# Blocks 2 and 3 of the last but one state: scaled by ScalarE and added by the adding transfer

## The chip, the cores and the metric

One core of a Trainium2 chip runs the whole program in one launch. Five engines work from queues of their own, each in order: TensorE (PE, matrix products and transposes, with weight loads PEld), VectorE (DVE), ScalarE (ACT), GpSimd (POOL) and SyncE (SP, which only issues transfers). They wait for each other through semaphores. The metric is device microseconds of one execution; smaller is better.

## What is computed

Four layers, each added to its input after a layer norm: attention, a dense layer with fp8 rounding, a selective state-space layer, and a mixture of eight experts with a shared one. The input is 16 sequences of 512 positions by 256 features. The change touches the state-space layer, in whose scan 512 inner channels carry 16 states each:

```python
def _selective_scan(u, delta, A, B_ssm, C_ssm):
    dA = jnp.exp(delta[..., None] * A)
    dBu = (delta * u)[..., None] * B_ssm[:, :, None, :]
    ...
    def step(h, inp):
        dA_i, dBu_i, c_i = inp
        h = dA_i * h + dBu_i
        y = jnp.einsum('bds,bs->bd', h, c_i)
        return (h, y)
    ...
y = _selective_scan(u, delta, A, B_ssm, C_ssm)
y = y + u * D_param
y = y * _silu(z)
out = y @ out_proj_w.T + out_proj_b
```

## The kernel before

**Turns.** One turn works on one sequence b: 16 states s, and for each state four scans m (128 channels by 512 positions each), so 64 scans n = 4s + m. Inside a turn's scans three streams of other work are woven in by a table of slots (AT): the late part of sequence b - 1 (its output projection, router and shared expert), the projections of b + 1, and the attention and fp8 layer of b + 2. What a stream has left over at the end of a turn is issued behind the last scan. A second program, the experts, follows the 16 turns.

**One state.** GpSimd multiplies dbu (L914) from du and a row of B that SyncE brings in; ScalarE takes the exponential into a bank (L1134); VectorE runs the scan h (L1505). When a state's four scans are done, TensorE transposes h into four blocks t of 128 positions by 512 channels (L697, called hT s.t), in banks 4 and 5 in turn: blocks 0 and 2 in bank 4, blocks 1 and 3 in bank 5. A bank is filled again only when the reader of its last content is done.

**Adding the states up.** acc holds four blocks; block t collects c times hT s.t over all states, where c is a column of cT. It starts as u times D (L687 on TensorE, L1125 on ScalarE). There are two ways to add:
- VectorE adds a block itself, from the bank (L1495, add_state). Blocks 0 and 1 of every state go so, and blocks 2 and 3 of the last two states.
- ScalarE scales a block into hTc (L1118, scale_state), and GpSimd, once blocks 2 and 3 of the state are scaled, sends one transfer of both (L900, send_scaled) that adds 128 x 1024 values of hTc onto acc. Blocks 2 and 3 of states 0 to 13 go so. hTc has room for one state (NSENT = 1), so the scaling of a state waits for the landing of the state before it; the semaphore sent counts the landings.

SENT, LAST_SENT, POOLED and KEPT at L28 to L30 say which (state, block) goes which way. Each addition of a block waits for the addition of the same block of the state before (acc_before); if that was a transfer, for its landing:

```python
elif (s - 1, t) in POOLED:
    sent_added(eng, b, s - 1)
```

**The end of a turn.** VectorE's additions stand five slots behind the scans (LAG), ScalarE's scalings too, and GpSimd's sends seven slots behind; those that don't fit into the 64 slots stand behind the loop. There, TensorE transposes state 15, VectorE adds its four blocks, and the streams are finished: ScalarE's copies L987 and L992, TensorE's L520, L527, L529 and L535, VectorE's L1476 and L1287. Then the late part of the sequence begins: TensorE transposes acc (L597, yT) when all of acc is added, VectorE multiplies by the gate (L1339), and TensorE projects (L609, L611). Then VectorE takes the statistics (L1222, L1227), from which GpSimd makes a chain of small operations (from L820), and the next turn's scans start. For them GpSimd has made the last of delta (L853), and du (L908) and dbu for four scans.

Of the kernel before, what the change touches and what calls it, by code (L numbers as in the profile page):

```python
# [11 lines left out]
NS = 16  # L12
# [12 lines left out]
NX2 = 3  # L25
STORE_AT = 10
ADDS = [(s, t) for s in range(NS) for t in range(TT)]
SENT, LAST_SENT, NSENT = (2, 3), NS - 2, 1  # L28
POOLED = [(s, t) for s, t in ADDS if t in SENT and s < LAST_SENT]
KEPT = [at for at in ADDS if at not in POOLED]  # L30

# [1722 lines left out]
```

## Time and profile before

| | us |
|---|---|
| median of 3 runs | 3189.42 |
| lowest, highest | 3184.73, 3194.21 |
| the profiled execution | 3189.66 |
| its span | 3188.0 |

| Engine | busy us | share of the span |
|---|---|---|
| TensorE | 2802.0 | 88% |
| VectorE | 2490.4 | 78% |
| GpSimd | 2158.0 | 68% |
| ScalarE | 2060.6 | 65% |

The busy share of an engine is an average over the turns and the experts, which differ: VectorE is nearly full in the turns and little used in the experts. The views that are read further on are groups of instructions (busy time, count, mean duration, idle time before them and what ended it), stretches of the span with each engine's busy time, and instructions in order of time. In those an instruction that waited carries in brackets how long its engine was idle and who ended that. Instructions of one line that follow each other at once are merged into one row, with their count behind the x.

### The profile page before, as it was taken

The numbers are of one execution on the slowest core, as the hardware profiler recorded it, in microseconds if no ns is written. First come the engines' busy times: TensorE is split into PE (matmuls) and PEld (weight loads), VectorE is DVE, ScalarE is ACT, GpSimd is POOL, SyncE is SP. The second block draws the span as 40 slices with busy tenths as digits, with TensorE's granted clock in tenths as the row PEclk, the third lists the DMA queues.
The fourth block names the chain that finished last, engine by engine and source line by source line (L and its number), as shares of the span: only waits on it lengthen the run. The fifth ranks groups of instructions, "written<-read, shape, count | busy, mean of one in ns | idle before, by whom it ended". The sixth has DMA issues, their size and how long they took to land. (4 is left out here: it accounts for less than half of the span.)

```text
span 3188.0 us, 47271 instructions
## 1 busy us (share of the span) xinstructions
PE 2802.0 (88%) x13224; PEld 1852.2 (58%) x13225; DVE 2490.4 (78%) x4116; ACT 2060.6 (65%) x3802; POOL 2158.0 (68%) x2205
## 2 busy tenths in 40 slices
PE   4777989898989898989989898989797789999998
PEld 2445555655655565656555555555555557777776
DVE  3599999999999999999999999999988632222222
ACT  3677777787777777777777777768665324444443
POOL 1378787787878687869687877877787524444443
PEclk8898999999999899999999999989998889999999
DMA  2043434343434343443434343434347324434433
GB/s 79 21 101 75 101 82 102 78 107 80 103 77 97 85 104 78 98 91 93 95 89 97 80 103 77 104 80 103 73 103 192 93 57 63 63 63 63 62 60 53
DMA packets 147644, 272.80 MB, mean 86 GB/s; under 512 B 19905, under 2 KB 78594, under 8 KB 147458
## 3 DMA queue, kind: packets, MB, share of 16 engines
q0 software_dynamic: 57984, 152.21, 26.9%
q1 hardware_dynamic: 79250, 109.78, 11.0%
q10 hardware_dynamic: 10224, 8.57, 0.8%
q8 instruction: 88, 1.44, 0.2%
q14 instruction: 98, 0.80, 0.1%
HBM read 107.29 MB, written 45.76 MB: 48 GB/s over the span
## 5 line engine op out<-in xcount | busy, mean ns | idle before, releaser
L914 POOL TENSOR_TENSOR dbu<-du,bbc 128x512 f32<-128x512 f32 x1024 | 1339.3, 1388 | 144.8 <-DVE h L1505 135.5
L1505 DVE TENSOR_TENSOR_SCAN h<-bank,dbu 128x512 f32<-128x512 f32 x1024 | 1220.6, 1210 | 51.8 <-ACT bank L1134 47.8
L1134 ACT ACTIVATE bank<-region,amat 128x512 f32<-128x512 f32 x1024 | 702.5, 689 | 99.2 <-DVE h L1505 94.1
L697 PE MATMUL bank<-ident,h 128*128 128x128 f32 x4096 | 623.7, 288 | 123.4 <-DVE acc L1495 54.3
L697 PEld LDWEIGHTS bank<-ident,h 128*128 128x128 f32 x4096 | 493.6, 147 | 406.6 <-issue 136.0
L1118 ACT ACTIVATE hTc<-bank,cT 128x512 f32<-128x512 f32 x448 | 306.2, 683 | 240.9 <-PE bank L697 131.5
L1672 POOL DMA_INDIRECT out<-ye,ids x136 | 213.7, 1571 | 347.7 <-DMA out<-ye,ids 305.7
L1495 DVE SCALAR_TENSOR_TENSOR acc<-bank,cT,acc 128x512 f32<-128x512 f32 x576 | 416.3, 730 | 21.8 <-PE bank L697 20.1
L651 PE MATMUL bank<-x4T,w_su 128*128 128x512 f32 (+1 forms) x768 | 376.4, 611 | 11.4 <-ACT region L961 10.2
L900 POOL DMA_DIRECT2D acc<-hTc x224 | 203.3, 908 | 268.8 <-ACT hTc L1118 256.5
L1708 DVE SCALAR_TENSOR_TENSOR gg<-gt,bank 128x352 f32<-128x352 f32 x136 | 71.1, 523 | 386.4 <-ACT gt L1642 386.4
L1609 PE MATMUL bank<-region,xeT 128*128 x1088 | 346.9, 462 | 1.5 <-ACT xeT L1638 1.5
L552 PE MATMUL bank<-region 128*128 128x512 f32 x512 | 270.0, 627 | 1.7 <-ACT region L1010 1.3
L577 PE MATMUL bank<-u,region 128*128 128x512 f32 x512 | 259.2, 600 | 13.8 <-ACT region L961 13.8
L1609 PEld LDWEIGHTS bank<-region,xeT 128*128 128x128 f32 x1088 | 197.0, 191 | 89.5 <-issue 3.9
L663 PE MATMUL bank<-w_sd,shh 128*128 128x256 f32 (+1 forms) x768 | 198.1, 392 | 12.6 <-DVE shh L1431 12.6
L651 PEld LDWEIGHTS bank<-x4T,w_su 128*128 128x128 f32 (+1 forms) x768 | 127.0, 188 | 127.9 <-issue 107.7
L1625 PE MATMUL bank<-region,hT 128*128 (+1 forms) x816 | 199.2, 380 | 1.6 <-ACT hT L1647 1.6
L663 PEld LDWEIGHTS bank<-w_sd,shh 128*128 128x128 f32 (+1 forms) x768 | 131.9, 189 | 65.0 <-issue 27.2
L887 POOL DMA_INDIRECT slots_in<-x,pos x128 | 130.5, 1020 | 56.7 <-issue 26.6
L479 PE MATMUL bank<-region 128*128 128x512 f32 x256 | 161.6, 759 | 2.5 <-ACT region L954 1.8
L1653 ACT ACTIVATE ye<-bank,slot_tag 128x256 f32<-128x256 f32 x136 | 64.4, 473 | 146.7 <-PE bank L1625 143.3
(222 smaller groups left out, 4259.1 us busy)
## 6 DMA issues: line engine op xcount, KB each, us to landing
acc<-hTc POOLq DMA_DIRECT2D x224, 512.0 KB, 4.8
bbc<-b_scratch SPq DMA_DIRECT2D x256, 256.0 KB, 3.5
xe<-slots_in SPq DMA_DIRECT2D x136, 129.0 KB, 2.6
region<-in_x SPq DMA_DIRECT2D x16, 512.0 KB, 3.8
out<-x ACTq DMA_DIRECT2D x16, 512.0 KB, 3.3
region<-in_e_gu SPq DMA_DIRECT2D x8, 704.0 KB, 6.2
out<-ye,ids POOLq DMA_INDIRECT x136, 4.1
slots_in<-dbu SPq DMA_DIRECT2D x16, 129.0 KB, 2.8
```

What stands on the lines that cost most here:

```text
L552: last = mm(proj[f"in{m}", b][:, :], w_in[:, c, m * P:(m + 1) * P], r4T[:, c, :], start=c == 0, stop=c == DC - 1)
L577: last = mm(proj[f"dt{m}", b][:, :], w_dt[:, k, m * P:(m + 1) * P], u[:, k, :], start=k == 0, stop=k == MC - 1)
L651: last = mm(late[f"{name}{n}", b][0:size, :], w_su[:, c, half * SI + at:half * SI + at + size], x4T[:, c, :], start=c == 0, stop=c == DC - 1)
L663: last = mm(late[f"d{k}", b][:, (j % 2) * D:(j % 2 + 1) * D], shh[0:size, n, j * P:(j + 1) * P], w_sd[0:size, n, :], start=n == 0, stop=n ...
L697: last = tr(scan[f"hT{s}.{t}"][:, m * P:(m + 1) * P], h[:, s % 2, m, t * P:(t + 1) * P], ident[:, :])
L914: g.tensor_tensor(dbu[:, n % 4, :], du[:, m, :], bbc[:, (b * NS + s) % NROW, :], ALU.mult).then_inc(S("dbu_ready"), 1)
L1118: f(hTc[:, s % NSENT, t - SENT[0], :], scan[f"hT{s}.{t}"][:, :], ACT.Copy, scale=cT[:, par, t, s:s + 1]).then_inc(S("scaled"), 1)
L1134: f(db(n)[:, :], delta[:, 1 - par, m, :], ACT.Exp, scale=amat[:, m, s:s + 1]).then_inc(S("da_ready"), 1)
L1495: v.scalar_tensor_tensor(acc[:, t, :], hT[:, :], c, acc[:, t, :], ALU.mult, ALU.add).then_inc(S("acc_ready"), 1)
L1505: v.tensor_tensor_scan(h[:, s % 2, m, :], db(n)[:, :], dbu[:, n % 4, :], 0.0, ALU.mult, ALU.add)\
L1609: last = mm(banks[2 * k + half][:, 0:I], xeT[:, k, c, :], w_gu[:, bass.ds(e, 1), c, half * I:(half + 1) * I].rearrange("p a n -> p (a n)") ...
L1672: g.indirect_dma_start(out, bass.IndirectOffsetOnAxis(ids[:, k:k + 1], 0), ye[:, k, :], None, compute_op=ALU.add)\
```

## The change

The adding transfer also takes blocks 2 and 3 of state 14. One constant is changed, and every list and wait that depends on it follows:

```diff
-SENT, LAST_SENT, NSENT = (2, 3), NS - 2, 1
+SENT, LAST_SENT, NSENT = (2, 3), NS - 1, 1
 POOLED = [(s, t) for s, t in ADDS if t in SENT and s < LAST_SENT]
 KEPT = [at for at in ADDS if at not in POOLED]
```

What stands in the queues moves at the end of each turn. In a row, a bracket names the semaphores that the instruction waits for: sent for the landing of the adding transfer, scaled for ScalarE's scalings, acc_ready for VectorE's adds, scan_full0 and scan_full1 for banks 4 and 5.

VectorE at the end of a turn, before; bank 4 holds block 0 or 2, bank 5 block 1 or 3. The first two adds are blocks 2 and 3 of state 14, the next four are state 15:

```order
866 L1505 SCALAR_TENSOR_TENSOR h<-bank7,dbu 128x512 [waits dbu_ready,da_ready]
867 L1495 SCALAR_TENSOR_TENSOR acc<-bank4,cT,acc 128x512 [waits sent,scan_full0]
868 L1495 SCALAR_TENSOR_TENSOR acc<-bank5,cT,acc 128x512 [waits sent,scan_full1]
869 L1495 SCALAR_TENSOR_TENSOR acc<-bank4,cT,acc 128x512 [waits acc_ready,scan_full0]
870 L1495 SCALAR_TENSOR_TENSOR acc<-bank5,cT,acc 128x512 [waits acc_ready,scan_full1]
871 L1495 SCALAR_TENSOR_TENSOR acc<-bank4,cT,acc 128x512 [waits acc_ready,scan_full0]
872 L1495 SCALAR_TENSOR_TENSOR acc<-bank5,cT,acc 128x512 [waits acc_ready,scan_full1]
873 L1476 SCALAR_TENSOR_TENSOR x4<-bank1,sg2,x2 128x256 [waits attn_proj_late_full1]
```

And after, at the same place:

```order
860 L1505 SCALAR_TENSOR_TENSOR h<-bank7,dbu 128x512 [waits dbu_ready,da_ready]
861 L1495 SCALAR_TENSOR_TENSOR acc<-bank4,cT,acc 128x512 [waits acc_ready,scan_full0]
862 L1495 SCALAR_TENSOR_TENSOR acc<-bank5,cT,acc 128x512 [waits acc_ready,scan_full1]
863 L1495 SCALAR_TENSOR_TENSOR acc<-bank4,cT,acc 128x512 [waits sent,scan_full0]
864 L1495 SCALAR_TENSOR_TENSOR acc<-bank5,cT,acc 128x512 [waits sent,scan_full1]
865 L1476 SCALAR_TENSOR_TENSOR x4<-bank1,sg2,x2 128x256 [waits attn_proj_late_full1]
```

Two adds are gone, and the wait for sent stands at blocks 2 and 3 of state 15 instead of state 14.

ScalarE at the same place, the piece of the difference: L1134 is the exponential for the turn's last scan, L987 the first of the copies behind the loop.

```order
 L983 ACTIVATE region<-bank3 128x1024
 L1134 ACTIVATE bank7<-region,amat 128x512
+L1118 ACTIVATE hTc<-bank4,cT 128x512
+L1118 ACTIVATE hTc<-bank5,cT 128x512
 L987 ACTIVATE region<-bank2,s_both 128x512
 L987 ACTIVATE region<-bank0,s_both 128x512
```

The two scalings of state 14 now stand ahead of the copies, for which TensorE's L527 waits.

GpSimd at the same place, before: the send of state 13, the last dbu of the turn, the last two of delta (L853), and the next turn's du and dbu.

```order
541 L900 DMA acc<-hTc 128x1024 [waits sent,scaled]
542 L914 TENSOR_TENSOR dbu<-du,bbc 128x512 [waits scan_done]
543 L853 TENSOR_TENSOR region<-region 128x512 [waits dt_ln] x2
544 L908 TENSOR_TENSOR du<-region,u 128x512 [waits delta_ready,dbu_ready]
545 L914 TENSOR_TENSOR dbu<-du,bbc 128x512 [waits scan_done,b_row2,du_ready]
```

And after:

```order
549 L900 DMA acc<-hTc 128x1024 [waits sent,scaled]
550 L914 TENSOR_TENSOR dbu<-du,bbc 128x512 [waits scan_done]
551 L853 TENSOR_TENSOR region<-region 128x512 [waits dt_ln]
552 L900 DMA acc<-hTc 128x1024 [waits sent,scaled]
553 L853 TENSOR_TENSOR region<-region 128x512 [waits dt_ln]
554 L908 TENSOR_TENSOR du<-region,u 128x512 [waits delta_ready,dbu_ready]
555 L914 TENSOR_TENSOR dbu<-du,bbc 128x512 [waits scan_done,b_row2,du_ready]
```

The send of state 14 stands between the last two of delta, ahead of all that GpSimd makes for the next turn. TensorE's and SyncE's queues hold the same instructions in the same order; only what they wait for differs.

## Rows read from the trace of the kernel before

**Rows 1.** The page's busy table: busy us, share of span, instructions.
```profile
PE 2802.0 (88%) x13224; PEld 1852.2 (58%) x13225; DVE 2490.4 (78%) x4116; ACT 2060.6 (65%) x3802; POOL 2158.0 (68%) x2205
```

**Rows 2.** Three whole turns: stretch, length, busy per engine, PEclk, DMA share, GB/s.
```profile
1187.10:1337.30 150.20, 135.19 (x665) 87.22 (x665) 144.00 (x228) 113.49 (x195) 119.64 (x120) 0.97 0.40 92
1034.40:1187.10 152.70, 137.42 (x665) 89.41 (x665) 144.41 (x228) 113.53 (x195) 119.56 (x120) 0.94 0.39 90
1788.60:1940.70 152.10, 137.61 (x665) 89.07 (x665) 144.04 (x229) 113.46 (x195) 119.39 (x120) 0.94 0.39 91
```

**Rows 3.** Line L1339: duration ns least/median/most, first and last start.
```profile
L1339 DVE TENSOR_TENSOR region<-bank,region x64: 679/682/693, 280.7 to 2526.6; 128x512 f32<-128x512 f32 x64
```

**Rows 4.** VectorE in order of time at one turn end: start, length, instructions.
```profile
876.09 1.39 DVE L1495 SCALAR_TENSOR_TENSOR acc<-bank,cT,acc 128x512 f32<-128x512 f32 x2
...
877.71 2.91 DVE L1495 SCALAR_TENSOR_TENSOR acc<-bank,cT,acc 128x512 f32<-128x512 f32 x4 [0.23 <-PE bank L697]
...
887.12 4.54 DVE L1505 TENSOR_TENSOR_SCAN h<-bank,dbu 128x512 f32<-128x512 f32 x4
```

**Rows 5.** Groups: count, busy us, mean ns, idle before and its releaser.
```profile
L1118 ACT ACTIVATE hTc<-bank,cT 128x512 f32<-128x512 f32 x448 | 306.2, 683 | 240.9 <-PE bank L697 131.5
...
L1495 DVE SCALAR_TENSOR_TENSOR acc<-bank,cT,acc 128x512 f32<-128x512 f32 x576 | 416.3, 730 | 21.8 <-PE bank L697 20.1
...
L900 POOL DMA_DIRECT2D acc<-hTc x224 | 203.3, 908 | 268.8 <-ACT hTc L1118 256.5
```

**Rows 6.** The other engines in order of time at the same turn end.
```profile
868.70 0.60 PE L697 MATMUL bank<-ident,h 128*128 128x128 f32 x4
869.34 0.69 ACT L1118 ACTIVATE hTc<-bank,cT 128x512 f32<-128x512 f32 x1 [0.46 <-PE bank L697]
...
870.33 0.89 POOL L900 DMA_DIRECT2D acc<-hTc  x1 [0.49 <-ACT hTc L1118]
...
870.96 1.57 POOL L914 TENSOR_TENSOR dbu<-du,bbc 128x512 f32<-128x512 f32 x1
...
872.19 2.78 POOL L853 TENSOR_TENSOR region<-region 128x512 f32<-128x512 f32 x2
...
874.64 1.57 POOL L908 TENSOR_TENSOR du<-region,u 128x512 f32<-128x512 f32 x1
...
875.27 1.09 PE L697 MATMUL bank<-ident,h 128*128 128x128 f32 x8
...
876.63 0.38 PE L527 MATMUL bank<-region,identb 128*128 128x512 bf16 x1
...
877.07 1.12 PE L697 MATMUL bank<-ident,h 128*128 128x128 f32 x8
...
884.04 1.27 POOL L914 TENSOR_TENSOR dbu<-du,bbc 128x512 f32<-128x512 f32 x1
...
887.28 0.20 POOL L820 TENSOR_TENSOR ve<-mv,eps 128x4 f32<-128x4 f32 x1 [1.97 <-DVE mv L1227]
```

**Rows 7.** L900's landing, all 224; and one send with the scaling that waited.
```profile
DMA to landing us min/median/max: 4.5/4.8/6.8
...
984.75 0.97 POOL L900 DMA_DIRECT2D acc<-hTc  x1 [1.08 <-issue]
...
989.68 0.69 ACT L1118 ACTIVATE hTc<-bank,cT 128x512 f32<-128x512 f32 x1 [3.33 <-DMA acc<-hTc]
```

**Rows 8.** Stretches of 4 us at turn ends and turn starts, columns as Rows 2.
```profile
434.80:438.80 4.00, 4.00 (x22) 3.81 (x22) 3.85 (x9) 2.47 (x4) 2.86 (x9) 0.73 0.55 185
...
886.60:890.60 4.00, 4.00 (x31) 3.78 (x30) 3.85 (x9) 2.70 (x5) 2.85 (x9) 1.00 0.57 185
...
1032.00:1036.00 4.00, 2.36 (x17) 1.66 (x16) 3.82 (x8) 1.79 (x3) 3.84 (x4) 1.00 0.02 6
...
2096.90:2100.90 4.00, 4.00 (x21) 3.76 (x21) 3.85 (x9) 2.47 (x4) 2.90 (x9) 0.71 0.55 196
```

## The prediction

> **What bounds the kernel now.** I read the busy table first, then the costliest groups, then one whole turn (the loop over one batch block: 16 states, four scans each), and last the instructions at the end of a turn. By the busy table [rows 1] TensorE is busy for 88% and VectorE for 78% of the span, but the span has two parts: the turns, up to about 2527 us, and the experts behind them. In a whole turn VectorE is busy for 144.00 of 150.2 us and TensorE for 135.19 [rows 2], and VectorE's idle time comes in pieces of a few tenths. So a turn is as long as VectorE's queue, and a delay in that queue is a delay of the kernel, unless a later wait of VectorE gives it back. The four multiplications of L1339 close each turn; there are 64 of them [rows 3], so 16 turn ends.
>
> The change acts only there. In the trace's order at one turn end [rows 4]: VectorE adds blocks 2 and 3 of state 14 (876.09, two adds), waits 0.23 us for the transposes of state 15, then adds the four blocks of state 15 from 877.71 to 880.62 (2.91 us, so 0.727 us each) with no gap. What follows in its queue is as tight, and the first scan of the next turn starts at 887.12. The other turn ends read alike.
>
> **What goes.** Two adds of 0.730 us [rows 5] a turn leave VectorE, 32 in all, 23.4 us of its time. They lie before that 0.23 us wait, and the wait grows into their place: VectorE can't add state 15 before state 15 is transposed, and that transpose needs the bank of block 2 of state 14 to be read, by whichever engine. So I value them at nothing on the path.
>
> **What comes.** 32 scalings on ScalarE at 0.683 us, 22 us, and 16 adding transfers whose issue holds GpSimd for 0.908 us each [rows 5], 15 us. Neither engine bounds a turn, so their busy time is worth nothing by itself. But there is a wait that was not there: the add of state 15's block 2 now waits for the transfer of state 14. Before, the same wait stood at block 2 of state 14, for the transfer of state 13, which had been issued at 870.33 [rows 6], 5.76 us before the add at 876.09, long enough. Now the transfer is issued late and its reader comes at once. Behind the waiting add in VectorE's queue stand the other add, the base adds of L1476, the x2 sums of L1287, the four multiplications of L1339, and the scans of the next turn; TensorE's yT transposes (L597) wait for it as well.
>
> **The chain, step by step.** TensorE's transposes of state 14's blocks 2 and 3 start at T = 875.27 and take 1.09 us together [rows 6]; nothing before them changes. From the start of such a transpose to its scaling it is 0.64 us (868.70 to 869.34), from the scaling's end to the send 0.30 us (870.03 to 870.33) [rows 6]. Block 3's transpose starts about 0.55 behind T, and its scaling stands behind block 2's on ScalarE, so it starts at about T + 1.2 and ends at T + 1.9; the send starts at T + 2.2, at 877.5. Landing takes 4.5, 4.8 or 6.8 us (least, median, most) from the issue, and an idle engine that waited for it starts 4.93 us after the send's start (984.75 to 989.68) [rows 7]. So block 2's add of state 15 starts at 877.5 + 4.93 = 882.4. Before it started at 877.71 + 2 x 0.727 = 879.16. **The turn end grows by 3.3 us**, 3.27 unrounded, and the 16 of them by 52 us. With the least landing, 0.3 less than the median, it is 3.0 and 48; with 6.8 it would be 5.2, but that is the worst case of 224 and not the rule.
>
> TensorE alone would cost less. ScalarE's two new scalings stand ahead of L987, and TensorE's L527 waits for the first L987; before it ran at 876.63 without a wait, 0.44 before the transposes of state 15 at 877.07 [rows 6]. Now L987 starts at about 877.1 and ends at 877.8, L527 follows, the transposes come at 878.2, the first add at 878.9, and block 2's transpose, which needs block 0's bank, is ready at about 880.6. That is 1.4 us later than 879.16 (22 us for 16), and the transfer at 882.4 covers it. Were ScalarE's scaling of block 3 itself late, both would move together.
>
> **GpSimd** is held longest, since the send stands in its queue ahead of the last delta and of the next turn's du and dbu. It went on at 872.19 with two L853, had du 0 at 874.64 and the last dbu of the first state at 884.04 [rows 6]. Now: send at 877.5, free 0.63 later (870.33 to 870.96), the last L853 takes 1.2, du 0 at 879.4, and 9.4 later, at 888.8, dbu 3 starts and is done at 890.0. The fourth scan, at 887.12 + 3 x 1.135 = 890.5 before, comes at 893.8 with the turn end 3.3 later, so it finds dbu 3. The chain of small operations from L820 began at 887.28, after waiting for VectorE's statistics [rows 6]; these come 3.3 later, at 890.6, when GpSimd is free again. I put the cost of these 5 us at nothing; the margin is 0.6 us at L820 and about 3.8 at the scan. If it's gone, each microsecond costs one.
>
> **TensorE's clock.** In the 4 us at the start of the next turn's dense work the granted clock is 1.00 (2.4 GHz) at 12 of 16 turn ends and 0.64 to 0.73, so in part at 1.2 GHz, at four; the first, one of those without, and the last are shown [rows 8]. Before one such fall, TensorE was busy for 2.36 of 4 us, at the turn end itself [rows 8]. The turns with a fall last 152.7 and 152.1 us, one without lasts 150.2 [rows 2]: 2.2 us more. The change adds 3.3 us in which TensorE has nothing to do just there, in two pieces (before state 15's transposes, and before yT). I expect the fall at 12 or so of the 16 instead of four: 8 more at 2.2 us, **18 us**. The bounds are 0 (no more falls) and 12 x 2.2 = 26, or 31 if each is a fifth longer. I take 18, nearer the upper one, since the turn ends with and without a fall look the same, so that 3.3 us more of idle time should tip most of them. The Trainium skill ("TensorE: Matmul & The Clock Gate", The HAM clock gate) says that a throttled clock is the default and that activity releases it; by that rule the fall should become regular here, and the rows with a fall after a thin stretch agree.
>
> The Trainium skill ("DMA: Bandwidth & Descriptors", on the fixed cost) puts a GpSimd-issued transfer at 2.0 us plus its bytes over 436 GB/s. For 512 KB that is an estimate of 3.2 us, where the trace has 4.8; by 3.2 the turn end would grow by 1.7 and the 16 by 27 us. The trace's duration is the one that I use.
>
> **The sum.** The profiled execution took 3189.66 us (span 3188.0), the median of three is 3189.42, so they stand for each other. 3189.7 + 52 + 18 = 3260 us. Nothing is taken off for a delay that a later wait gives back: VectorE's waits in the turn are for TensorE and ScalarE, which themselves wait for VectorE at the turn end and so move along.
>
> **Rivals.**
> (1) The wait costs 3.3 us but TensorE's clock falls no more often: 3189.7 + 52 = 3242. For it: a turn end with the same idle as the falling ones mostly kept its clock.
> (2) Part of the wait is hidden. Either the transfer lands faster with VectorE and the queues quiet, so that TensorE's 1.4 us decide (22 us), or later waits of VectorE give half of the 3.3 us back (26 us): 3212 to 3216. Against it: least landing of 224 is 4.5 us.
> (3) Faster: the delays of the turn end are all given back in the turn, and VectorE's 23.4 us count in full: 3189.7 - 23.4 = 3166 us. That decides as soon as VectorE's idle in a turn (6.2 us of 150.2 [rows 2]) holds over 3.3 us that don't move with the turn end. Against it: those pieces are for engines that are released by VectorE itself.
> (4) No effect, within 0.3%: the transfer lands by 879.2, where block 2 was added before, and TensorE isn't held either. It would have to land within 1.7 us of its issue, and no row shows that.
> (5) Worse than my sum: GpSimd's margin at L820 is gone, or transfers land at 5.5 us and more, and the clock falls everywhere, over 3284 us.
>
> **How the numbers follow.** The sum with more falls of the clock 50%, (1) 27%, (2) 13%, (3) 2%, (4) 3%, (5) 5%. The likeliest is 3260. The range is 3228 to 3284: below, half-way from (1) to (2); above, the 48 to 58 us of waiting and the upper bound of the clock. About 0.3%, 9.6 us, is what a measurement of this kernel can tell from no change. Faster by more 0.03, within 0.03, slower 0.94.
>
> **What would show it.** After: VectorE's first add of state 15 some 3 us after scan 63 ended, then an idle of about 1.5 to 2 us before the third add, put down to the transfer's landing, 16 times; the first scan of a turn starting 3.3 us later against scan 63; GpSimd's send at the turn end waiting 5 us for ScalarE; 240 transfers and 480 scalings, 544 adds; granted clock at the next turn's start under 1.00 in most turns, and full turns of 153 to 156 us. I am wrong if the third add is released by TensorE, if GpSimd's dbu holds the scans, or if the turns grow by other than 3 to 5.5 us; and for the opposite sign, if they get shorter than 150.

## The result, and the profile after

The changed kernel takes 3262.39 us (median of 4 runs, 3257.75 to 3265.89) where the kernel before takes 3187.07 us in the same comparison (4 runs, 3178.96 to 3194.21): 1.024 times as long, 95% interval 1.0223 to 1.0257. It is slower, by 75 us; 3260 had been predicted. Its profiled execution has a span of 3260.7 us, 72.7 more than the 3188.0 of before, so the traces carry nearly all of it.

The page of the kernel after, busy table and the groups that answer to [rows 1, 5]:

```profile
PE 2834.8 (87%) x13224; PEld 1876.2 (58%) x13225; DVE 2476.0 (76%) x4084; ACT 2079.2 (64%) x3834; POOL 2171.7 (67%) x2221
...
L1118 ACT ACTIVATE hTc<-bank,cT 128x512 f32<-128x512 f32 x480 | 326.4, 683 | 272.8 <-PE bank L697 167.8
L1495 DVE SCALAR_TENSOR_TENSOR acc<-bank,cT,acc 128x512 f32<-128x512 f32 x544 | 394.6, 730 | 104.6 <-PE bank L697 68.8
L900 POOL DMA_DIRECT2D acc<-hTc x240 | 217.3, 906 | 334.9 <-ACT hTc L1118 331.3
```

The work moved as announced: 32 adds fewer (576 to 544), 32 scalings and 16 transfers more, at the same durations. The reader should not stop at VectorE's busy time, which fell by 14.4 us. The column to read is the idle time before the adds: 21.8 us before the change, 104.6 after. The line's own waits say who ended it (us, times):

```profile
  PE bank L697: 68.8, 44
  DMA acc<-hTc: 34.3, 16
```

Sixteen waits for the landing, one per turn end, 2.1 us each. The wait for TensorE's transposes grew as well, from 20.1 to 68.8 us: the two adds that used to fill the time ahead of state 15 (23.4 us) are gone, and the transposes themselves come later (the first add of state 15 starts 3.88 us behind the start of scan 63 on average instead of 2.75, 18 us for 16).

One turn end of the kernel after in order of time (start, length, engine, line, in brackets the idle time and its releaser), to be laid beside [rows 4, 6]; the first row is the turn's last scan, scan 63:

```profile
1047.32 1.21 DVE L1505 TENSOR_TENSOR_SCAN h<-bank,dbu 128x512 f32<-128x512 f32 x1
1047.63 1.09 PE L697 MATMUL bank<-ident,h 128*128 128x128 f32 x8
1048.32 1.27 ACT L1118 ACTIVATE hTc<-bank,cT 128x512 f32<-128x512 f32 x2 [2.20 <-PE bank L697]
1049.48 1.27 ACT L987 ACTIVATE region<-bank,s_both 128x512 bf16<-128x512 f32 x2
1049.89 0.86 POOL L900 DMA_DIRECT2D acc<-hTc  x1 [3.78 <-ACT hTc L1118]
1050.22 0.39 PE L527 MATMUL bank<-region,identb 128*128 128x512 bf16 x1 [1.06 <-ACT region L987]
1050.67 1.04 PE L697 MATMUL bank<-ident,h 128*128 128x128 f32 x8
1051.31 1.41 DVE L1495 SCALAR_TENSOR_TENSOR acc<-bank,cT,acc 128x512 f32<-128x512 f32 x2 [2.77 <-PE bank L697]
...
1054.50 1.41 DVE L1495 SCALAR_TENSOR_TENSOR acc<-bank,cT,acc 128x512 f32<-128x512 f32 x2 [1.78 <-DMA acc<-hTc]
1055.96 1.09 PE L597 MATMUL bank<-ident,acc 128*128 128x128 f32 x8 [1.02 <-DVE acc L1495]
1057.93 1.28 DVE L1339 TENSOR_TENSOR region<-bank,region 128x512 f32<-128x512 f32 x2
1063.03 0.20 POOL L820 TENSOR_TENSOR ve<-mv,eps 128x4 f32<-128x4 f32 x1 [0.67 <-DVE mv L1227]
```

Counted from the start of scan 63: the first add of state 15 at +3.99 (held by L527, which waits for L987), the send at +2.57, the third add at +7.18 (held by the landing), the first L1339 at +10.61. Before, the first L1339 stood at +7.68 at most turn ends. L820 still waits for VectorE, so GpSimd is not late.

The granted clock is the other half. Two stretches of 4 us at a turn start of the kernel after (columns as [rows 8]), one at full clock and one at 0.50, so at 1.2 GHz, and three whole turns (as [rows 2]):

```profile
1532.30:1536.30 4.00, 4.00 (x31) 3.78 (x31) 3.85 (x9) 2.77 (x5) 3.30 (x10) 1.00 0.67 196
1061.90:1065.90 4.00, 4.00 (x19) 3.76 (x19) 3.85 (x9) 2.15 (x4) 2.86 (x10) 0.50 0.51 172
...
1213.90:1371.40 157.50, 138.91 (x665) 89.90 (x665) 143.14 (x226) 114.70 (x197) 121.17 (x121) 0.93 0.40 91
1528.30:1682.80 154.50, 136.65 (x665) 87.52 (x665) 142.73 (x226) 114.55 (x197) 120.53 (x121) 0.96 0.41 93
1682.80:1840.60 157.80, 140.38 (x665) 91.38 (x665) 143.26 (x227) 114.50 (x197) 120.61 (x121) 0.92 0.40 91
```

In four microseconds TensorE ran 31 matmuls or 19. I call it a fall when the granted clock is under 0.95 in the 8 us behind a turn's first L1339: 4 of 16 before, 13 of 16 after.

### The profile page after: what moved, and what is told of

It is laid out like the page before. It is cut to its first block and busy times, and to the rows that moved or that the text cites. A ratio compares the mean times of both kernels' runs of the same rounds, so it can differ in the third digit from the quotient of the medians.

```text
span 3260.7 us, 47287 instructions
## 1 busy us (share of the span) xinstructions
PE 2834.8 (87%) x13224; PEld 1876.2 (58%) x13225; DVE 2476.0 (76%) x4084; ACT 2079.2 (64%) x3834; POOL 2171.7 (67%) x2221
## 5 line engine op out<-in xcount | busy, mean ns | idle before, releaser
L1134 ACT ACTIVATE bank<-region,amat 128x512 f32<-128x512 f32 x1024 | 702.3, 689 | 92.1 <-DVE h L1505 89.2
L697 PE MATMUL bank<-ident,h 128*128 128x128 f32 x4096 | 620.8, 287 | 121.7 <-DVE acc L1495 51.6
L697 PEld LDWEIGHTS bank<-ident,h 128*128 128x128 f32 x4096 | 493.2, 147 | 402.9 <-DVE acc L1495 135.4
L1118 ACT ACTIVATE hTc<-bank,cT 128x512 f32<-128x512 f32 x480 | 326.4, 683 | 272.8 <-PE bank L697 167.8
L1495 DVE SCALAR_TENSOR_TENSOR acc<-bank,cT,acc 128x512 f32<-128x512 f32 x544 | 394.6, 730 | 104.6 <-PE bank L697 68.8
L900 POOL DMA_DIRECT2D acc<-hTc x240 | 217.3, 906 | 334.9 <-ACT hTc L1118 331.3
```

Source lines behind the costliest of these rows:

```text
L697: last = tr(scan[f"hT{s}.{t}"][:, m * P:(m + 1) * P], h[:, s % 2, m, t * P:(t + 1) * P], ident[:, :])
L1118: f(hTc[:, s % NSENT, t - SENT[0], :], scan[f"hT{s}.{t}"][:, :], ACT.Copy, scale=cT[:, par, t, s:s + 1]).then_inc(S("scaled"), 1)
L1134: f(db(n)[:, :], delta[:, 1 - par, m, :], ACT.Exp, scale=amat[:, m, s:s + 1]).then_inc(S("da_ready"), 1)
L1495: v.scalar_tensor_tensor(acc[:, t, :], hT[:, :], c, acc[:, t, :], ALU.mult, ALU.add).then_inc(S("acc_ready"), 1)
```

## The experiments

Positions are counted from the start of scan 63, as above. "First L1339" is the mean over the 16 turn ends; the next column is the mean over 15 turn ends of the time from there to the next turn's first scan (behind the last there is none); "full turn" is the mean length of 12 turns, each measured from its predecessor's first L1339 to its own; the first of these stretches and the last two, which hold less work, are left out. "Clock" is the granted clock over the whole span, as a share of full speed, averaged over the timed runs. The positions, the falls and the full turn come from one profiled execution each; time, ratio, interval and clock come from the timed runs. Kernels with the same letter were timed together and share the runs of the kernel before (a: 3188.88 us, b: 3188.47, c: 3186.57); a and b ran on one chip, c on another. "after" in an edit's first line means that it is made on the changed kernel, "before" on the old one.

| kernel | us | ratio [95%] | first L1339 | to the next scan | falls | full turn | clock |
|---|---|---|---|---|---|---|---|
| before | 3187.07 | | 7.49 | 4.37 | 4 | 151.4 | 0.944 to 0.945 |
| after | 3262.39 | 1.0240 [1.0223, 1.0257] | 10.73 | 4.78 | 13 | 156.2 | 0.932 |
| after_again (a) | 3262.70 | 1.0229 [1.0203, 1.0255] | 10.62 | 4.79 | 12 | 156.2 | 0.932 |
| unsent (a) | 3212.82 | 1.0068 [1.0041, 1.0095] | 8.69 | 4.37 | 7 | 153.2 | 0.942 |
| copy_first (a) | 3275.79 | 1.0269 [1.0243, 1.0295] | 10.70 | 5.08 | 16 | 156.9 | 0.923 |
| fill (a) | 3254.69 | 1.0218 [1.0187, 1.0248] | 10.49 | 4.52 | 8 | 155.0 | 0.939 |
| unheld (b) | 3209.87 | 1.0074 [1.0053, 1.0096] | 8.63 | 4.37 | 3 | 152.5 | 0.942 |
| split (b) | 3257.31 | 1.0218 [1.0200, 1.0237] | 9.94 | 4.70 | 9 | 155.6 | 0.932 |
| base_early (b) | 3246.50 | 1.0182 [1.0161, 1.0204] | 10.03 | 4.64 | 7 | 154.7 | 0.936 |
| ns3 (b) | 3216.85 | 1.0085 [1.0058, 1.0113] | 7.96 | 4.37 | 1 | 153.3 | 0.944 |
| copy_fill (c) | 3264.96 | 1.0250 [1.0233, 1.0267] | 10.64 | 4.60 | 8 | 155.0 | 0.935 |
| before_base_early (c) | 3179.17 | 0.9977 [0.9964, 0.9991] | 7.39 | 4.37 | 0 | 150.5 | 0.948 |
| three (c) | 3906.77 | 1.2255 [1.2219, 1.2290] | | | | | 0.882 |
| rows2 (c) | 3190.46 | 1.0012 [0.9999, 1.0024] | | | | | 0.944 |

The theories: **landing**, the third add of state 15 waits for the transfer of state 14; **TensorE**, the scalings ahead of L987 hold state 15's transposes and that decides the turn end; **GpSimd**, the held send delays dbu; and **clock**, the added idle time makes the granted clock fall more often at the turn's start.

**The kernel after again.** No edit; it shows how far an execution stands for the kernel.

> The changed kernel itself, unedited, as the yardstick for the other three on the same chip. Every theory expects about 1.024 of the kernel before (some 75 us more), with the third add of state 15 about 7.2 us after the start of the turn's last scan, released by the transfer's landing, and a granted clock under 1.00 at the start of most turns.

The ratio agrees, and the two traces have 13 and 12 falls and 10.73 and 10.62 for the first L1339. So a difference of one or two falls says nothing. The scatter can be larger still: unsent and unheld below have the same turn end, the same time and the same clock in the timed runs (0.942), but 7 and 3 falls in their one traced execution. Where falls are compared, the clock of the timed runs is the firmer number.

**The transfer of state 14 left out.** ScalarE's scalings, their place ahead of L987 and GpSimd's wait for them stay; only the send is gone, so blocks 2 and 3 of state 14 are missing from the sum.

```diff
@@ after: send_scaled
                     if s == 0:
                         for block in SENT:
                             done(pool, "acc_init", b, block)
+                    if s == LAST_SENT - 1:
+                        return
                     sent_added(pool, b, s - 1)
@@ sent_added
+            sends = LAST_SENT - 1
-            if b * LAST_SENT + s >= 0:
-                eng.wait_ge(sent, 16 * (b * LAST_SENT + s + 1))
+            if b * sends + s >= 0:
+                eng.wait_ge(sent, 16 * (b * sends + min(s, sends - 1) + 1))
```

> The changed kernel with the transfer of state 14 left out (its blocks 2 and 3 are scaled but never added, so two blocks of one state are missing from the sum). GpSimd still waits for ScalarE's scalings at the same place. Landing theory (mine): the third add of state 15 is released by TensorE at about 5.4 us after the start of the last scan instead of 7.2 or more (before: 4.2), so 16 x 1.2 = 19 us remain, and perhaps half of the 25 us that the clock costs: 3205 to 3225 us, 40 to 55 less than the changed kernel. Rival (the two scalings ahead of ScalarE's copies, or GpSimd's held queue, set the turn end): at least 60 of the 75 us stay, 3245 us or more.

50 us of the 75 are gone (3262.70 to 3212.82). The same turn end in its trace: all four adds of state 15 run on behind TensorE's transposes (L698 here is L697 of the others, L1498 is L1495, L1342 is L1339).

```profile
1040.12 1.22 DVE L1508 TENSOR_TENSOR_SCAN h<-bank,dbu 128x512 f32<-128x512 f32 x1
...
1044.10 2.92 DVE L1498 SCALAR_TENSOR_TENSOR acc<-bank,cT,acc 128x512 f32<-128x512 f32 x4 [2.77 <-PE bank L698]
...
1049.04 1.28 DVE L1342 TENSOR_TENSOR region<-bank,region 128x512 f32<-128x512 f32 x2
```

The first L1339 stands at +8.92 instead of +10.61. What is left over before, 1.20 us per turn end (8.69 less 7.49), is TensorE's share: 19 us for 16, and with three more falls about 25, where the span grew by 27 (3215.4 less 3188.0). Landing and TensorE are thus both real, one behind the other.

**GpSimd's wait left out too.** The same return, ahead of the wait for the scalings:

```diff
@@ after: send_scaled
                     if (s, t) not in POOLED or t != SENT[-1]:
                         return
+                    if s == LAST_SENT - 1:
+                        return
                     done(pool, "scaled", b, POOLED.index((s, t)))
```

> As the run without the transfer of state 14 (its blocks 2 and 3 are scaled but not added), and GpSimd no longer waits for ScalarE's scalings at the turn end either. Landing theory: GpSimd's hold costs nothing, so the time is that of the run without the transfer, about 3213 us or 1.007 of the kernel before, within 5 us, and the turn end is the same 8.7 us from the last scan's start to the first L1339. Rival (GpSimd's held queue delays the next turn's scans): 10 us or more less than with the hold.

1.0074 against 1.0068: no difference. Holding GpSimd for some 4 us at each turn end costs nothing that these runs can tell, which is to about 0.3%.

**Copies ahead of the scalings.** On ScalarE the first of the two copies L987, the one that L527 and the transposes of state 15 wait for, goes ahead of the last scalings; the second stays behind them.

```diff
@@ after: ScalarE's loop over the scans
-                    if n >= LAG:
+                    if n >= LAG and n < UNITS - 1:
                         scale_state(*divmod(n - LAG, TT))
                     issue(streams, n - 1)
-                for k in range(UNITS - LAG, UNITS):
+                issue(streams, UNITS - 1)
+                for k in range(UNITS - 1 - LAG, UNITS):
                     scale_state(*divmod(k, TT))
```

> The changed kernel with ScalarE's first copy L987 ahead of the two scalings of state 14 instead of behind them, so that TensorE's L527 and the transposes of state 15 are not held. Landing theory: the first two adds of state 15 start about 1.1 us earlier, the third does not (7.2 us after the last scan's start, or up to 0.1 later), and the time is that of the changed kernel within 5 us. Rival (ScalarE's copies hold TensorE and that sets the turn end): 16 x 1.1 = 17 us less than the changed kernel.

The TensorE theory alone would have it faster, the landing theory the same. At one turn end:

```profile
1055.34 1.22 DVE L1506 TENSOR_TENSOR_SCAN h<-bank,dbu 128x512 f32<-128x512 f32 x1
...
1058.09 1.41 DVE L1496 SCALAR_TENSOR_TENSOR acc<-bank,cT,acc 128x512 f32<-128x512 f32 x2 [1.53 <-PE bank L697]
...
1062.52 1.41 DVE L1496 SCALAR_TENSOR_TENSOR acc<-bank,cT,acc 128x512 f32<-128x512 f32 x2 [3.02 <-DMA acc<-hTc]
...
1063.99 1.09 PE L597 MATMUL bank<-ident,acc 128*128 128x128 f32 x8 [2.26 <-DVE acc L1496]
...
1065.95 1.28 DVE L1340 TENSOR_TENSOR region<-bank,region 128x512 f32<-128x512 f32 x2
```

The first two adds come 1.24 us sooner, at +2.75, and everything from the third add, +7.18, is where it was: with the transfer there, TensorE is not what ends the turn. But the kernel is 13 us slower than after_again (3271.73 to 3278.97 us against 3259.39 to 3266.96), which neither theory had. The turn end up to L1339 is the same (10.70), all 16 turn starts have a fall, the clock of the timed runs is lower in every one (0.922 to 0.924 against 0.931 to 0.934), and the time from L1339 to the next scan grew to 5.08. The TensorE idle time that the change brought lies in the kernel after in two pieces of about 1 us (ahead of L527 and ahead of L597), and here in one piece of 2.26 us ahead of L597. L597's mean duration shows what follows; the rows are those of before, after and copy_first:

```profile
L597 PE MATMUL bank<-ident,acc 128*128 128x128 f32 x256 | 36.8, 280 | 18.1 <-DVE region L1339 16.4 <-DVE acc L1495 1.7
```

```profile
L597 PE MATMUL bank<-ident,acc 128*128 128x128 f32 x256 | 46.7, 338 | 46.1 <-DVE acc L1495 25.1 <-DVE region L1339 20.9
```

```profile
L597 PE MATMUL bank<-ident,acc 128*128 128x128 f32 x256 | 58.0, 402 | 57.0 <-DVE acc L1496 42.6 <-DVE region L1340 14.3
```

280, 338, 402 ns for the same matmul. The last two multiplications of L1339 wait for these transposes, so part of a fall is paid at the turn end itself: 4.37, 4.78 and 5.08 us to the next scan.

**Matmuls in TensorE's gaps.** Eight dummy matmuls ahead of the wait for L987, seven ahead of the last L535; their result is overwritten by the next one in the bank.

```diff
@@ after: TensorE, ahead of L527 (k == 0) and of L535 (k == 1)
+                    if k == 0:
+                        attn.may_fill(pe, f"biased{k}", b, done)
+                        for _ in range(8):
+                            mm(attn[f"biased{k}", b][:, 0:D], identb[:, :], kq[:, 0, :], start=True, stop=True)
                     done(pe, "yb_ready", b, k)
-                    attn.may_fill(pe, f"biased{k}", b, done)
+                    if k == 1:
+                        attn.may_fill(pe, f"biased{k}", b, done)
@@
+                    for _ in range(7 * k):
+                        mm(attn[f"y{k}", b][:, 0:D], identb[:, :], kq[:, 0, :], start=True, stop=True)
```

> The changed kernel with 15 extra small bf16 matmuls of TensorE at each turn end (8 ahead of the first L527, 7 ahead of the second L535, about 0.11 us each, into a bank that the next matmul overwrites), where TensorE is idle for about 1 us each time. Clock theory: the third add stays at 7.2 us, the clock at the start of the next turn stays 1.00 in most turns, and the full turns get 1 to 2 us shorter: 15 to 25 us less than the changed kernel, 3237 to 3247 us. Rival (the falls have another cause, or cost nothing): the same time as the changed kernel, or up to 5 us more for the added work.

Falls went from 12 or 13 to 8 and L1339-to-scan from 4.8 to 4.52; the time fell by 8 us, less than the 15 to 25 expected, and the intervals of the ratios overlap. The clock of the timed runs rose in all four (0.935 to 0.941 against 0.931 to 0.934), and within them the time goes with it: 3251.07 and 3252.32 us at 0.941, 3257.07 at 0.937, 3264.97 at 0.935. In this execution a full turn with a fall took 156.04 us on average and one without 153.91, 2.1 us apart, as before (152.80 and 150.66).

**The same for copy_first**, with 18 dummy matmuls in its one long gap:

```diff
@@ copy_first: ahead of L535 (k == 1)
+                    for _ in range(18 * k):
+                        mm(attn[f"y{k}", b][:, 0:D], identb[:, :], kq[:, 0, :], start=True, stop=True)
```

> The kernel with ScalarE's first copy ahead of the scalings (3276 us, with a fall of the clock at every turn start), plus 18 small bf16 matmuls of TensorE ahead of the second L535, in the single idle stretch of over 2 us that stands before the yT transposes there. Clock theory: the falls at the turn starts go back to half or fewer of the turns, the turn end stays at 10.6 us from the last scan's start to L1339, and the time drops by 15 to 30 us, to 3246 to 3261. Rival (copying first costs 13 us for another reason than the clock): 3270 us or more.

In its trace the gap ahead of the yT transposes is down to 0.30 us:

```profile
1059.17 2.14 PE L536 MATMUL bank<-kq,identb 128*128 128x256 bf16 x18 [0.47 <-ACT region L994]
...
1061.83 1.09 PE L599 MATMUL bank<-ident,acc 128*128 128x128 f32 x8 [0.30 <-DVE acc L1498]
```

Falls 16 to 8, L1339-to-scan 5.08 to 4.60, first L1339 unmoved (10.64), time down from 3275.79 to 3264.96. The two ran on different chips; by their ratios (1.0269 and 1.0250) the gain is 6 us rather than 11, the intervals overlap, and 3246 to 3261 us had been expected. The size of the gain is thus not settled. The clock is clearer: 0.933 to 0.938 in the four timed runs against 0.922 to 0.924. In both filled kernels nothing was changed but what TensorE does while it waits. That its idle time at the turn end lowers the clock is shown by this; that the time follows is supported, less firmly.

**The transfer in two.** Blocks 2 and 3 of state 14 are sent each on its own, the first as soon as it is scaled, and the add of block 2 waits for the first alone.

```diff
@@ after: send_scaled
+                    if s == LAST_SENT - 1 and t in SENT:
+                        done(pool, "scaled", b, POOLED.index((s, t)))
+                        if t == SENT[0]:
+                            sent_added(pool, b, s - 1)
+                        k = t - SENT[0]
+                        g.dma_start(acc[:, t:t + 1, :], hTc[:, s % NSENT, k:k + 1, :], accum_op=ALU.add).then_inc((sent2, sent)[k], 16)
+                        return
@@ acc_before
+            elif (s - 1, t) == (LAST_SENT - 1, SENT[0]):
+                eng.wait_ge(sent2, 16 * (b + 1))
@@ scale_state
+                        if s == 0 and b > 0:
+                            act.wait_ge(sent2, 16 * b)
```

> The changed kernel with state 14's transfer cut into two of 256 KB, block 2 sent as soon as it is scaled and block 3 behind it, each waited for by the add of its own block. Landing theory: block 2 is sent 0.6 to 0.7 us earlier and lands no later than 4.6 us after that, so the third add starts at 6.2 to 6.6 us after the last scan's start instead of 7.2 and the fourth at about 7.2; the turn end shrinks by 0.6 to 0.8 us, 10 to 13 us in all, and with a few falls of the clock less 3245 to 3253 us. Rival (the size or number of transfers does not matter because something else releases the add): no change, 3262 us, or more by the second issue on GpSimd.

```profile
1045.95 1.22 DVE L1516 TENSOR_TENSOR_SCAN h<-bank,dbu 128x512 f32<-128x512 f32 x1
...
1047.94 1.76 POOL L900 DMA_DIRECT2D acc<-hTc  x2 [3.20 <-ACT hTc L1129]
...
1049.93 2.25 DVE L1506 SCALAR_TENSOR_TENSOR acc<-bank,cT,acc 128x512 f32<-128x512 f32 x3 [2.77 <-PE bank L699]
1052.87 0.75 DVE L1506 SCALAR_TENSOR_TENSOR acc<-bank,cT,acc 128x512 f32<-128x512 f32 x1 [0.69 <-DMA acc<-hTc]
```

The send starts at +1.99 and block 2's add needs no wait any more here; where it does wait, at +5.97 (so 3.98 behind the send). The add of block 3 waits at +6.92. The first L1339 typically comes at +9.7, 0.9 sooner, but at other turn ends block 3 lands as late as +8.2; the mean gain is 0.7 us a turn end, 11 us for 16. The timed runs fell by only 5 us against after_again, less than the 9 to 17 expected. The two traces differ by 10 us (spans 3255.0 and 3265.3), as the turn ends say, so the scatter of single executions may be all that is missing; it isn't settled.

**The base add sooner.** The two L1476 that stand behind the adds of state 15 (0.86 us together) move ahead of them, into VectorE's wait for their transposes. It was tried on both kernels:

```diff
@@ after, before: VectorE's steps
-                steps += [(AT["fin"][k], 2, base_of, k) for k in range(2)]
+                steps += [((AT["fin"][0], UNITS - 0.5)[k], 2, base_of, k) for k in range(2)]
@@
                 for k in range(UNITS - LAG, UNITS):
+                    if k == UNITS - TT:
+                        issue(streams, UNITS - 0.5)
                     add_state(*divmod(k, TT))
```

> The changed kernel with VectorE's two base adds of L1476 (0.87 us) ahead of the four adds of state 15 instead of behind them, where VectorE is idle for 2.8 us. Landing theory: the third add stays at 7.2 us after the last scan's start, and the first L1339 comes 0.87 us earlier at 15 of 16 turn ends (turn 0 has no such adds): 13 us less, 3249 us, up to 8 less still if the clock falls less often since TensorE waits less between its yT transposes. Rival (VectorE's turn end is bound by TensorE's yT and not by its own queue behind the landing): 3262 us.

> The kernel before with VectorE's two base adds of L1476 ahead of the four adds of state 15. There VectorE idles for only 0.23 us, so by the landing theory nothing is to be had: the first L1339 within 0.2 us of where it was, and the time within 6 us of the kernel before. Rival (moving these adds helps by itself, not by filling a wait): 13 us less than before, as the same edit gave in the changed kernel.

On the changed kernel 16 us of the 75 come back: the wait becomes useful work, typically 0.9 us at a turn end, and the falls drop to 7. On the old kernel, where only 0.23 us of waiting was to be filled, it brings 7 us, one more than the 6 expected at most, ratio 0.9977 [0.9964, 0.9991], the fastest of all kernels here. The turn end gains only 0.1 us there, 2 us for 16. The rest goes with the falls, none instead of four, and with the clock of the timed runs, 0.948 instead of 0.945; that it is the clock's doing was not tested by itself. TensorE's idle time up to the first L1339 is the same (about 1.25 us), but behind it TensorE works more densely. The rows (columns as [rows 8]) are the stretch that lies to this turn end as 1032.00:1036.00 lies to its own, 3.02 of 4 us busy where that has 2.36, and the 4 us behind the first L1339, where the kernel before is busy for 2.39:

```profile
1030.52:1034.52 4.00, 3.02 (x22) 2.06 (x21) 3.75 (x7) 1.79 (x3) 3.86 (x4) 1.00 0.04 5
1033.00:1037.00 4.00, 2.62 (x20) 2.05 (x19) 3.83 (x9) 0.07 (x2) 2.73 (x3) 1.00 0.43 137
```

**One state fewer sent**, the change made backwards:

```diff
@@ before
-SENT, LAST_SENT, NSENT = (2, 3), NS - 2, 1
+SENT, LAST_SENT, NSENT = (2, 3), NS - 3, 1
```

> The kernel before with the cut one state earlier the other way: blocks 2 and 3 of state 13 too are added by VectorE, 32 adds more, and ScalarE's 32 scalings and 16 transfers less. Theory: VectorE bounds the turns and nothing at the turn end waits for a transfer there, so the adds cost their 0.73 us each in full: 23 us more than the kernel before, 3210 to 3214 us or 1.007, with the turn end itself unchanged. Rival (VectorE's time in a turn has slack, or the last transfer's landing costs something before as well): within 8 us of the kernel before.

28 us slower than before, a little over the 3210 to 3214 us expected. 32 more adds of 0.730 us are 23.4 us, and inside a turn VectorE pays them in full. The first L1339 is 0.47 us later on average (7.5 us for 16), which wasn't foreseen: at three turn ends VectorE waited for TensorE until +2.79 with block 2 of state 14, and the four adds of state 15 came at +4.5 instead of +2.85. With three falls fewer the sum is about 25. So sending is worth what VectorE saves as long as the reader of the block is far enough away, and the change before us went one state too far.

**Three blocks sent**, with room made by two row buffers instead of three, and the kernel with that alone:

```diff
@@ before
-NROW = 3
+NROW = 2
-SENT, LAST_SENT, NSENT = (2, 3), NS - 2, 1
+SENT, LAST_SENT, NSENT = (1, 2, 3), NS - 2, 1
```

> The other direction: ScalarE scales and the transfer adds blocks 1, 2 and 3 of states 0 to 13 (384 of 512 positions), and only two rows of B are kept in SBUF instead of three for want of room. VectorE's adds fall by 14 a turn, 10 us of its 144. If VectorE's busy time were all that counts: 16 x 10 = 160 us less, 3030 us. By the landing theory ScalarE can't scale block 1 of a state until the transfer of the state before has landed, now 768 KB and sent one block later, with the exponentials for the scans queued behind: 1 to 3 us of wait for each of 14 states a turn, 16 x 14 x 1 to 3 = 220 to 670 us, less the 160: slower than before, 3250 to 3700 us.

> The kernel before with two rows of B in SBUF instead of three, as the yardstick for the run with three blocks. A row is loaded in about 3.5 us and used for some 9, so no theory expects a change: within 8 us of the kernel before.

The row buffer costs nothing (1.0012). Three blocks cost 22.6%, more than the 3250 to 3700 us expected. The waits of that trace, all over the turns (engine, line, for whom: us in total, times, longest):

```profile
POOL acc L900 <- ACT hTc L1118: 855.2, 218, 8.3
ACT hTc L1118 <- DMA acc<-hTc: 776.3, 195, 6.9
DVE h L1505 <- ACT bank L1134: 458.4, 208, 6.3
```

```profile
DMA to landing us min/median/max: 5.7/6.3/7.9
```

With one buffer of scaled blocks, ScalarE can't scale the next state's block 1 before the transfer has landed. The row above is the landing (least, median, most): 6.3 us for three blocks instead of 4.8 for two, and of a state's four blocks only one isn't sent, so the next block to be scaled follows closely. ScalarE waits 776 us (195 waits of 4.0 us on average, where 1 to 3 us had been put), its exponentials wait behind that, and VectorE's scans for them. It is the same wait that the change brought to the turn end, now in every state.

## Why the prediction was right

**The direction and the mechanism** held as put: the third add of state 15 is released by the landing, 16 times. With that count rival (4) falls, and rival (2) in its first form, in which the landing is hidden. That later waits give the delay back, half of it in (2) or all of it in (3), is answered by the spans: they grew by 72.7 us, and the turns inside got no shorter. Rival (5) has two halves: GpSimd's margin held, and late landings came at four of 16 turn ends only.

**The turn end** was put at 3.27 us, 52 for 16; the first L1339 moved by 3.24 on average, 52. Small errors cancel in it. The add started 4.61 us behind the send (1049.89 to 1054.50), not 4.93, so a typical turn end grew by 2.93 only (+7.68 to +10.61). But at four turn ends the transfer landed later, with the add at +7.7 to +8.5 against the +7.18 of most (this trace has no landing times; in after_again the longest at a turn end is 6.1 us), and the last two turn ends, at which no L527 runs, grew by 3.5. I had taken the median landing for all 16 and named the worst case as a bound.

**TensorE's own 1.4 us**, covered by the transfer, measured 1.20 in unsent, where it is uncovered; copy_first showed that it decides nothing while the transfer is there. **GpSimd's zero** is shown by unheld beside unsent, and by L820 which still waits 0.67 us for VectorE, where 0.6 was predicted. GpSimd's wait for ScalarE ahead of the send was 3.78 us, not 5, which only eases it.

**The clock** was put at 8 more falls and 18 us. It was 9 more falls. The span grew by 72.7; less the 52 of the turn ends that leaves 21. Of these 6 lie between L1339 and the next scan (0.41 x 15), in L597 at the lower clock, 11 between the first and the last scan of the turns, and 4 behind the last L1339, in the experts, whose start has a fall too (there the span runs on for 667.1 us instead of 663.4). The prediction had the whole of it in the turns. That rival (1), no more falls, was wrong is shown by the counts; that a fall costs about 2 us rests on turns with and without one within a kernel (152.80 and 150.66 before, 156.38 and 155.32 after, where only two of the 12 had none; 156.74 and 154.67 in after_again). The fills changed only TensorE's idle time and moved clock and time together, the time by little more than its scatter.

One reading of the prediction carries less than it was given. The thin stretch before a fall, 2.36 of 4 us, is no sign of a fall: the same stretch stands at turn ends of the kernel before that kept their clock (columns as [rows 8]):

```profile
1184.69:1188.69 4.00, 2.36 (x17) 1.65 (x16) 3.81 (x8) 1.79 (x3) 3.84 (x4) 1.00 0.06 7
```

So that 8 more turns would fall was a guess between 0 and 12, and that it came to 9 is in part luck. Two smaller things: the full turns last 154.6 to 157.7 us, a little over the 153 to 156 put as a sign; and the upper end of the range, 3284 us, doesn't come out of its own terms, since 3189.7 + 58 + 31 gives 3279.

What stays open: why a transfer of the same size lands 0.5 to 1.3 us later at some turn ends (no other large transfer is the reason: in the 8 us behind the send all transfers together move 66 GB/s at the turn end shown and 68 at two of the late ones, and at the last turn end 198 without being late); whether split really gave back half of what its turn ends saved; what the 18 us of the clock would be if only the clock were changed; and what exactly decides between a turn with and without a fall, since turn ends that look alike differ.

## What to carry to other kernels

A sum handed to an adding transfer is free only while its reader is farther away than scaling, issue and landing together, here 2.6 us from the start of the turn's last scan to the send and 4.6 from there to the add; the last item before the sum is read should stay on the engine that reads it. When an engine's work is taken away next to a wait, first ask what the wait becomes: 23.4 us of adds were saved and the idle time ahead of the remaining adds grew by 83 us (21.8 to 104.6). If some wait must stay at such a place, put independent work of the same engine into it: that brought 16 of 75 us back here, and 7 us even in the kernel before.

## What was not expected of the hardware

- The same idle time cost more in one piece. With TensorE's gaps at the turn end joined into one of 2.26 us, all 16 turn starts had the lower clock (13 and 12 with two gaps of about 1 us), the clock over the timed runs was 0.923 instead of 0.932, and the kernel took 13 us longer at an unchanged turn end.
- An adding transfer's time grew less than its size: in split a reader of one block (128x512 f32, 256 KB) started 3.98 us behind the send, that of two blocks 4.61 in the kernel after; landings took 4.2 us in the median for 256 KB (split), 4.8 us for 512 KB (before) and 6.3 us for 768 KB (three).
- A program that loses no time to the clock at its turn starts can be had by moving two instructions of 0.86 us together: in before_base_early falls went from 4 of 16 to none, and the clock over the timed runs from 0.945 to 0.948.
